# Cross attention of a perceiver block: scores laid out as [key, query] in a ring of seven chunks

## The chip, the cores and the metric

The kernel runs on one core of a Trainium2 chip. The metric is the device time of one launch in microseconds (us). The engines are named as the profile names them: PE (TensorE), DVE (VectorE), ACT (ScalarE), POOL (GpSimd) and SP (the queue that issues the DMAs).

## The reference, cut to what matters

A perceiver block: cross attention of 2 x 128 query tokens over 2 x 2048 context tokens, then self attention, then a feed-forward layer with one of four experts for each token. Everything is float32. The change touches only the first line.

```python
# x: (2, 128, 512)   ctx: (2, 2048, 512)   16 heads of 32
q = split_heads(layernorm(x) @ Wq + bq)
k = split_heads(ctx @ Wk + bk)
v = split_heads(ctx @ Wv + bv)
scores = einsum('bhqd,bhkd->bhqk', q, k) / sqrt(32)
attn = softmax(scores, axis=-1)                  # over 2048 keys
x = x + einsum('bhqk,bhkd->bhqd', attn, v) ... @ Wo + bo
x = x + self_attention(layernorm(x))             # not touched
x = x + ffn(layernorm(x))                        # not touched
```

## The kernel before, in words

Each engine has its own program, written out by hand in one block (`block.tensor`, `block.vector`, `block.scalar`, `block.gpsimd`, `block.sync`); semaphores with constant counts tie them together. An engine works strictly in the order of its program.

The cross attention works in passes `p` = 0 to 7: sample `b = p // 4` and head group `g = p % 4`, four heads to a group. A pass goes over `C` = 4 chunks of 512 keys; chunk number `n = 4p + c` runs from 0 to 31. For a chunk PE does the following:

- `keys` (its products are recorded at L720, in `product`): 12 matmuls of 512 columns make the keys of the four heads from the context, whose float32 values are split in a high and a low part. DVE adds the bias and puts them in `Kr` (L458).
- `scores` (L761): one matmul for each head with the queries stationary. The result is [query, key], 128x512 for a head, in PSUM banks 0 to 3. DVE (`negative_scores`, L478) copies it negated into `Pm` and carries a running minimum of each query, a value of its partition.
- After the four chunks of a pass ACT (`exponentials`, L317) takes the exponent over 2048 keys at once, with the maximum as a bias of the partition, and sums it on the way into `den`.
- `probs_T` (L775): 16 transposes for each chunk turn the probabilities into [key, query]. ACT copies three heads of each chunk into `PT` (L325), DVE the fourth (L487).
- `weighted_values` (L790): 16 matmuls with the values of 32 columns stationary, one column group of PE for each head. `reciprocals_T` (L798), a copy by ACT (L333) and `outputs` (L506, L508) on DVE divide by the sum and write `attnT`.
- `values` (also L720): 48 matmuls for a chunk make the values of all heads. This is done once for a sample: for sample 0 beside pass 0's chunks, for sample 1 in one piece after pass 3 (`if p == G`).

PE interleaves pass `p`'s keys and scores with pass `p - 1`'s transposes and weighted values. POOL splits the context of sample 1 (cast L290, subtraction L292), each chunk as soon as SP has loaded it; SP loads it once PE has used sample 0's chunk for the last time. POOL clears `KM` (L295) after the last weighted values. Then PE multiplies `attnT` by `Wo` (first product from 360.5 us in the profile), and the self attention and the feed-forward layer follow. DVE's step that adds the output's bias row (L567) waits for its row in `rowsA`.

Records: one float32 matmul stands in the trace as two (x2), a transpose and a matmul in the split form as one.

Of the kernel before, what the change touches and what calls it, by code (L numbers as in the profile page):

```python
# [23 lines left out]
def perceiver_block(nc, a, out):  # L24
# [23 lines left out]
    with ExitStack() as ctx:  # L48
# [220 lines left out]
        def _(pool):  # L269
            pool.memset(ident[:], 0.0).then_inc(ident_done, 1)  # L270
            pool.memset(minus_half, -0.5).then_inc(half_done, 1)
# [14 lines left out]
            pool.wait_ge(v_mm, C * JT)  # L286
            for c in range(C):

                pool.wait_ge(raw_in[c], 32)
                pool.tensor_copy(ctxH[c][:], raw[c][:]).then_inc(ctx_hi1, 1)  # L290
                pool.wait_ge(ctx_hi1, c + 1)
                pool.tensor_tensor(ctxL[c][:], raw[c][:], ctxH[c][:].bitcast(F32), ALU.subtract).then_inc(ctx_split1, 1)  # L292

            pool.wait_ge(pv_mm, NP * C)
# [743 lines left out]
```

## Time and profile before

| | |
|---|---|
| runs shown | 608.54, 610.73, 613.24 us; median 610.73 us |
| the profiled execution | 611.93 us, span 610.2 us |
| PE, busy | 540.0 us (88%) |
| DVE, busy | 306.8 us (50%) |
| ACT, busy | 156.8 us (26%) |
| POOL, busy | 35.6 us (6%) |
| mean granted clock of PE | 0.929 of full speed |

The span goes from the first to the last instruction; the run's own time is 1.7 us longer. Busy shares are averages over stages with different limits, so the stage that the change touches, from about 40 to 360 us, has to be read by itself.

### The profile page before, as it was taken

The page shows a single profiled execution, that of the slowest core. Times are in us where ns is not written, and L with a number is a line of the kernel's source. Part 1 is how long each engine was busy: PE and PEld are TensorE (multiplying, and loading weights), DVE is VectorE, ACT ScalarE, POOL GpSimd, SP SyncE. Part 2 cuts the span into 40 slices and gives each one's busy share as a digit, 9 for nine tenths or more (in the row PEclk, how much of TensorE's full clock was granted, in tenths as well). Part 3 has the DMA queues.
Part 4 walks back from the last instruction along what each step waited for, and adds up shares of the span by engine and source line. Part 5 has one row for each costly group of instructions (what it writes and reads, how often), then busy time and mean ns, then how long its engine had stood idle before and what let it go on. Part 6 is the DMA issues. An engine that isn't in the chain of part 4 may idle for free.

```text
span 610.2 us, 8249 instructions
## 1 busy us (share of the span) xinstructions
PE 540.0 (88%) x3378; PEld 389.9 (64%) x3378; DVE 306.8 (50%) x541; ACT 156.8 (26%) x229; POOL 35.6 (6%) x30
## 2 busy tenths in 40 slices
PE   1999999999989899999998778955875999999995
PEld 1777777777767688777775543422735688888642
DVE  6355435556666411175757133184366669766122
ACT  2010034647363431136373610012101100000400
POOL 0000000001950000000000020000000000000000
PEclk9999999999999999999999678975785599999998
DMA  8300000003400000300006240440130475553000
GB/s 355 161 1 0 2 0 2 1 2 118 160 1 3 1 0 1 137 3 2 1 1 275 106 139 1 103 106 0 22 116 0 188 295 165 212 184 129 1 1 33
DMA packets 24620, 46.18 MB, mean 76 GB/s; under 512 B 17540, under 2 KB 17540, under 8 KB 20356
## 3 DMA queue, kind: packets, MB, share of 16 engines
q1 hardware_dynamic: 24584, 45.66, 21.2%
q8 instruction: 27, 0.44, 0.3%
q14 instruction: 9, 0.07, 0.0%
HBM read 43.04 MB, written 2.62 MB: 75 GB/s over the span
## 4 chain that ended last, share of the span: by engine, by line
PE 82%; DVE 9%; DMA 3%; issue 3%; ACT 2%; POOL 0%; POOLq 0%; DVEq 0%; ACTq 0%
PE ps L720 42%; PE ps L775 10%; PE ps L761 6%; PE ps L971 5%; PE ps L790 5%; PE ps L972 5%; PE ps L973 5%; PE ps L906 1%; PE ps L960 1%; DMA qkvp<-qkv_dram 1%; DMA wk_raw<-in_xWk 1%; DVE Pm L478 1%; ACT Pm L317 1%; DVE small L436 1%; PE ps L714 1%
## 5 line engine op out<-in xcount | busy, mean ns | idle before, releaser
L325 ACT COPY PT<-ps 128x512 f32<-128x512 f32 x96 | 53.3, 588 | 99.9 <-PE ps L775 99.9
L775 PE MATMUL ps<-ident,Pm 128*128 128x128 f32 x512 | 72.0, 284 | 3.9 <-ACT PT L325 2.2
L775 PEld LDWEIGHTS ps<-ident,Pm 128*128 128x128 f32 x512 | 58.4, 144 | 24.3 <-issue 16.9
L478 DVE TENSOR_SCALAR_CACHE_REDUCE Pm<-ps,small 128x512 f32<-128x512 f32 x96 | 66.4, 748 | 8.6 <-PE ps L761 8.6
L317 ACT ACTIVATE Pm<-Pm,small 128x2048 f32<-128x2048 f32 x32 | 64.2, 2006 | 14.2 <-DVE Pm L478 14.2
L720 PE MATMUL ps<-ctxH,wkH 128*128 128x512 f32 x128 | 54.0, 422 | 15.3 <-DVE ctxL L450 12.8
L720 PE MATMUL ps<-ctxL,wkH 128*128 128x512 f32 x128 | 51.2, 400 | 0.0
L720 PE MATMUL ps<-ctxH,wkL 128*128 128x512 f32 x128 | 50.9, 398 | 0.0
L971 PE MATMUL ps<-w1H,zH 128*128 128x512 f32 x128 | 50.8, 397 | 0.0
L973 PE MATMUL ps<-w1H,zL 128*128 128x512 f32 x128 | 50.5, 395 | 0.0
L972 PE MATMUL ps<-w1L,zH 128*128 128x512 f32 x128 | 50.5, 395 | 0.0
L720 PE MATMUL ps<-wvH,ctxH 128*128 128x512 f32 x128 | 50.0, 391 | 0.0
L720 PE MATMUL ps<-wvH,ctxL 128*128 128x512 f32 x128 | 49.8, 389 | 0.0
L720 PE MATMUL ps<-wvL,ctxH 128*128 128x512 f32 x128 | 49.8, 389 | 0.0
L458 DVE TENSOR_SCALAR Kr<-ps,small 128x512 f32<-128x512 f32 x32 | 24.0, 750 | 49.2 <-PE ps L720 49.2
L720 PEld LDWEIGHTS ps<-ctxH,wkH 128*128 128x128 f32 x128 | 24.5, 192 | 34.0 <-issue 29.1
L467 DVE COPY V<-ps 128x512 f32<-128x512 f32 x16 | 11.1, 692 | 66.6 <-PE ps L720 66.6
L487 DVE COPY PT<-ps 128x512 f32<-128x512 f32 x32 | 22.1, 692 | 36.7 <-PE ps L775 35.9
L761 PE MATMUL ps<-Kr,qT 32*128 32x512 f32 x256 | 36.5, 640 | 0.6 <-ACT qT L344 0.6
L632 DVE TENSOR_TENSOR w1L<-w1raw,w1H 128x2048 fp32r<-128x2048 f32 x16 | 36.7, 2293 | 0.6
L790 PE MATMUL ps<-PT,V 128*32 128x128 f32 x1024 | 34.9, 277 | 0.9 <-DVE PT L487 0.9
L630 DVE CAST w1H<-w1raw 128x2048 fp32r<-128x2048 f32 x16 | 19.6, 1224 | 24.4 <-PE ps L973 24.4
(138 smaller groups left out, 677.8 us busy)
## 6 DMA issues: line engine op xcount, KB each, us to landing
w1raw<-in_W SPq DMA_DIRECT2D x16, 1024.0 KB, 4.8
raw<-in_ctxT SPq DMA_DIRECT2D x8, 1024.0 KB, 5.8
woF<-in_ffn_Wo SPq DMA_DIRECT2D x1, 4096.0 KB, 14.9
rows<-in_rows SPq DMA_DIRECT2D x8, 256.0 KB, 4.9
qkv_dram<-qkvn SPq DMA_DIRECT2D x2, 768.0 KB, 3.6
qkvp<-qkv_dram SPq DMA_DIRECT2D x2, 768.0 KB, 5.8
wk_raw<-in_xWk SPq DMA_DIRECT2D x1, 1024.0 KB, 4.8
wv_raw<-in_xWv SPq DMA_DIRECT2D x1, 1024.0 KB, 8.5
```

Source lines behind the costliest of these rows:

```text
L317: act.activation(Pm[:, i, :], Pm[:, i, :], ACT.Exp, bias=mx[:, p % 2, i, C - 1:C], scale=-1.0, accum_out=den[:, p, i:i + 1]).then_inc(exp_ ...
L325: act.copy(PT[:, c % 2, i, :, :].rearrange("p k t -> p (k t)"), ps[:, T_BANKS[i % 2], :]).then_inc(pt_act, 1)
L458: dve.tensor_scalar(Kr[:, c, :], ps[:, K_BANK, :], bias3[:, 1, p % G:p % G + 1], None, ALU.add).then_inc(k_done, 1)
L478: dve.tensor_scalar(Pm[:, i, c * CH:(c + 1) * CH], ps[:, i, :], -1.0, mx[:, p % 2, i, c - 1:c] if c else NOT_YET, ALU.mult, ALU.min, accum ...
L632: dve.tensor_tensor(w1L[n % 2][:], w1raw[n % 2][:], w1H[n % 2][:].bitcast(F32), ALU.subtract).then_inc(w1_split, 1)
L720: mm = pe.matmul(dst, l, r, start=(n == 0), stop=(n == len(pairs) - 1))
L761: pe.matmul(ps[:, i, :], qT[q, g, b * T:(b + 1) * T], Kr[q, c, :], start=True, stop=True)\
L775: last = pe.transpose(ps[:, T_BANKS[i % 2], j * P:(j + 1) * P], Pm[:, i, c * CH + j * P:c * CH + (j + 1) * P], ident[:])
L790: last = pe.matmul(ps[q, PV_BANK, 0:T], V[:, c * JT + j, (HPG * g + i) * DH:(HPG * g + i + 1) * DH], PT[:, c % 2, i, j, :], start=(c == 0 ...
L971: pe.matmul(dst, zH[:, n, t], wH[:, cc], start=False, stop=False)
L972: pe.matmul(dst, zH[:, n, t], wL[:, cc], start=False, stop=False)
L973: last = pe.matmul(dst, zL[:, n, t], wH[:, cc], start=False, stop=(n == NW1 - 1))
```

## The change

The work of a chunk is laid out as [key, query], so that the probabilities need no transposes.

- PE `scores`: the keys are stationary, 128 of them at a time, and the 128 queries of a head move: 16 matmuls of 128 columns for a chunk in place of 4 of 512. ACT, not DVE, copies the result into one of seven buffers `Sm` (8 KB each per partition), and ACT, not DVE, adds the bias to the keys; `Kr` has two buffers.
- The maximum of a query now lies over partitions. DVE `running_max` reduces a chunk's four blocks of 128 keys by a strided view into [128 keys, head, query] and takes the maximum with the chunks before. At the end of a pass PE transposes it (`maxima_T`), DVE reduces it to one value a query and head (`maxima`), PE spreads it over all partitions (`maxima_rows`, four matmuls with a broadcast column as weights), and ACT copies it to `mb`.
- DVE `subtract` takes `mb` from a whole chunk (128x2048), ACT takes the exponent of the chunk in place, PE multiplies it with the values.
- The sums of the probabilities: in the passes of `POOLED` POOL adds a chunk's four blocks into `acc` (three adds for chunk 0 of a pass, four for chunks 1 and 2), and PE adds chunk 3 and `acc` over the partitions with `ones` as weights (20 matmuls). In passes 2 and 7 PE does it all with `ones` (16 matmuls more a chunk). DVE takes the reciprocal of 128 columns.
- All engines now go through slots `n` = 0 to 37. In slot `n` PE makes scores `n`, keys `n + 1` and weighted values `n - 6`; ACT takes the exponent of `n - 6` and copies scores `n`; DVE takes the maximum of `n - 1` and subtracts for `n - 5`. The values of sample 1 are made in slots 19 to 22, one chunk in each.
- `acc` and `tmp` lie where `x` lay, so SP loads `x` again near the end of the stage.

The core of the diff:

```diff
-PT = at("PT", [P, 2, HPG, JT, T], F32, 160)
-Kr = at("Kr", [P, C, CH], F32, 176)
+NS = 7
+Sm = [at(f"Sm{n}", [P, HPG, JT, T], F32, 128 + 8 * n) for n in range(NS)]
+Kr = at("Kr", [P, 2, CH], F32, 184)
+run = at("run", [P, HPG, T], F32, 188)
+mb = at("mb", [P, HPG, T], F32, 190)
+acc = at("acc", [P, HPG, T], F32, 192)
+tmp = at("tmp", [P, HPG, T], F32, 194)
 x = at("x_sb", [P, B, D], F32, 192)
 qT = at("qT", [P, G, TOK], F32, 196)
 attnT = at("attnT", [P, G, TOK], F32, 200)
 ident = at("ident", [P, P], F32, 204)
 RT = at("RT", [P, T], F32, 204.5)
...
 NP = B * G
-NOT_YET = 3.0e38
+NCH = NP * C
+LAG = 6
+M_BANK, DEN_BANK = T_BANKS
+V1_SLOT = (G - 1) * C + LAG + 1
+POOLED = (0, 1, 3, 4, 5, 6)
...
+def pooled(n):
+    return n // C in POOLED and n % C < C - 1
+def denominator(p):
+    return ps[:, PV_BANK, P:2 * P] if p in POOLED else ps[:, DEN_BANK, 0:T]
+def sums_through(n):
+    return sum(pooled(k) for k in range(n + 1))
+def sums_before(p):
+    return sum(q < p for q in POOLED)
...
         sp.dma_start(w1raw[n][:], w1_v[n]).then_inc(w1_in[n], 16)
-    sp.wait_ge(s_mm, NP * C * HPG)
+    sp.wait_ge(s_mm, NCH * HPG)
     for n in range(2):
         sp.dma_start(rowsA[:, n, :], a["rows"][n:n + 1, :].to_broadcast([P, D])).then_inc(rowsA_in, 16)
+    sp.wait_ge(mT_mm, NP)
+    sp.wait_ge(den_mm, len(POOLED))
+    sp.dma_start(x[:], a["x"].rearrange("b t d -> t b d")).then_inc(x_in, 16)
+    sp.wait_ge(pv_mm, NCH)
     sp.dma_start(wr[:], a["W_router"]).then_inc(wr_in, 16)
-    sp.wait_ge(pv_mm, NP * C)
     for n in range(8):
         sp.dma_start(rows[:, n, :], a["rows"][2 + n:3 + n, :].to_broadcast([P, D])).then_inc(rows_in, 16)
...
+    steps = [0]
+    def denominators(n):
+        t = Sm[n % NS]
+        before = sums_through(n) - 1
+        pool.wait_ge(exp_done, n + 1)
+        if before:
+            pool.wait_ge(summed, before)
+        if n % C == 0:
+            if sums_before(n // C):
+                pool.wait_ge(den_mm, sums_before(n // C))
+            pool.tensor_tensor(acc[:], t[:, :, 0, :], t[:, :, 1, :], ALU.add).then_inc(add_step, 1)
+            steps[0] += 1
+        else:
+            for j in range(2):
+                pool.tensor_tensor(acc[:], acc[:], t[:, :, j, :], ALU.add).then_inc(add_step, 1)
+                steps[0] += 1
+                if j == 0:
+                    pool.wait_ge(add_step, steps[0])
+        pool.wait_ge(add_step, steps[0])
+        pool.tensor_tensor(acc[:], acc[:], t[:, :, 2, :], ALU.add).then_inc(add_step, 1)
+        steps[0] += 1
+        pool.wait_ge(add_step, steps[0])
+        pool.tensor_tensor(acc[:], acc[:], t[:, :, 3, :], ALU.add).then_inc(summed, 1)
+    for n in range(NCH):
+        if n == 2 * C:
+            pool.wait_ge(v_mm, C * JT)
+            for c in range(C):
+                pool.wait_ge(raw_in[c], 32)
+                pool.tensor_copy(ctxH[c][:], raw[c][:]).then_inc(ctx_hi1, 1)
+                pool.wait_ge(ctx_hi1, c + 1)
+                pool.tensor_tensor(ctxL[c][:], raw[c][:], ctxH[c][:].bitcast(F32),
+                                   ALU.subtract).then_inc(ctx_split1, 1)
+        if pooled(n):
+            denominators(n)
...
+    def keys(n):
+        g = n // C % G
+        act.wait_ge(k_mm, n + 1)
+        if n >= 2:
+            act.wait_ge(s_mm, (n - 1) * HPG)
+        act.activation(Kr[:, n % 2, :], ps[:, K_BANK, :], ACT.Identity, bias=bias3[:, 1, g:g + 1],
+                       scale=1.0).then_inc(k_done, 1)
...
+    def scores(n):
+        if n >= NS:
+            act.wait_ge(pv_mm, n - NS + 1)
+            if pooled(n - NS):
+                act.wait_ge(summed, sums_through(n - NS))
+            if (n - NS) % C == C - 1 and (n - NS) // C in POOLED:
+                act.wait_ge(den_mm, sums_before((n - NS) // C) + 1)
+        for i in range(HPG):
+            act.wait_ge(s_mm, n * HPG + i + 1)
+            act.copy(Sm[n % NS][:, i, :, :].rearrange("p j t -> p (j t)"), ps[:, i, :]).then_inc(s_done, 1)
+    def maxima(p):
+        act.wait_ge(mB_mm, p + 1)
         if p:
...
+            act.wait_ge(sub_done, C * p)
+        act.copy(mb[:].rearrange("p h t -> p (h t)"), ps[:, M_BANK, :]).then_inc(mb_done, 1)
+    def exponentials(n):
+        act.wait_ge(sub_done, n + 1)
+        t = Sm[n % NS][:].rearrange("p h j t -> p (h j t)")
+        act.activation(t, t, ACT.Exp).then_inc(exp_done, 1)
+    act.wait_ge(bias_in, 16)
...
+    for n in range(NCH + LAG):
+        if n >= LAG:
+            exponentials(n - LAG)
+        if n < NCH:
+            scores(n)
+        if C < n <= NCH + 1 and n % C == 1:
+            maxima(n // C - 1)
+        if n + 1 < NCH:
+            keys(n + 1)
+        if n + 1 < C:
+            for j in (0, 2):
+                values(0, n + 1, j)
...
+    def running_max(n):
+        t = Sm[n % NS]
+        dve.wait_ge(s_done, HPG * (n + 1))
+        dst = tmp if n % C else run
+        if n:
+            dve.wait_ge(run_ready, n)
+        red = dve.tensor_reduce(dst[:], t[:].rearrange("p h j t -> p h t j"), AX.X, ALU.max)
+        if n % C == 0:
+            red.then_inc(run_ready, 1)
+            return
+        run_steps[0] += 1
+        red.then_inc(run_step, 1)
+        dve.wait_ge(run_step, run_steps[0])
+        dve.tensor_tensor(run[:], run[:], tmp[:], ALU.max).then_inc(run_ready, 1)
+    def maxima(p):
+        dve.wait_ge(mT_mm, p + 1)
+        dve.tensor_reduce(mq, ps[:, M_BANK, :].rearrange("p (h t) -> p h t", h=HPG), AX.X, ALU.max)\
+           .then_inc(m_ready, 1)
+    def subtract(n):
+        t = Sm[n % NS]
+        dve.wait_ge(mb_done, n // C + 1)
+        dve.tensor_tensor(t[:], t[:], mb[:].rearrange("p h (o t) -> p h o t", o=1).to_broadcast([P, HPG, JT, T]),
+                          ALU.subtract).then_inc(sub_done, 1)
     def outputs(p):
         b, g = divmod(p, G)
         dst = attnT[:, g, b * T:(b + 1) * T]
...
         dve.wait_ge(pv_mm, C * (p + 1))
...
+        if p in POOLED:
+            dve.wait_ge(den_mm, sums_before(p) + 1)
+        dve.reciprocal(RT[:], denominator(p)).then_inc(o_step, 1)
+        dve.wait_ge(o_step, 2 * p + 1)
+        dve.tensor_tensor(dst, ps[:, PV_BANK, 0:T], RT[:], ALU.mult).then_inc(o_step, 1)
+        dve.wait_ge(o_step, 2 * p + 2)
         dve.tensor_scalar(dst, dst, bias3[:, 2, g:g + 1], None, ALU.add).then_inc(o_done, 1)
...
+    for n in range(NCH + LAG):
+        if n + 1 < C:
+            if n + 2 < C:
+                split(n + 2)
+            for j in (1, 3):
+                values(0, n + 1, j)
+        if 0 <= n - 1 < NCH:
+            running_max(n - 1)
+        if n >= C and n % C == 0 and n <= NCH:
+            maxima(n // C - 1)
+        if n - LAG >= C and (n - LAG) % C == 0:
+            outputs((n - LAG) // C - 1)
+        if 0 <= n - (LAG - 1) < NCH:
+            subtract(n - (LAG - 1))
+        if 0 <= n - V1_SLOT < C:
+            for j in (1, 3):
+                values(1, n - V1_SLOT, j)
     outputs(NP - 1)
...
         t = slice(j * P, (j + 1) * P)
         product(ps[:, T_BANKS[j % 2], :], [(l[:, k, t], w[:, k, :]) for k in range(KT)
                                            for l, w in ((ctxH[c], wvH), (ctxH[c], wvL), (ctxL[c], wvH))])\
...
+    def scores(n):
+        b, g = divmod(n // C, G)
         pe.wait_ge(k_done, n + 1)
+        for j in range(JT):
+            for i in range(HPG):
+                q = slice(DH * i, DH * (i + 1))
+                if n and j == 0:
+                    pe.wait_ge(s_done, (n - 1) * HPG + i + 1)
+                mm = pe.matmul(ps[:, i, j * P:(j + 1) * P], Kr[q, n % 2, j * P:(j + 1) * P],
+                               qT[q, g, b * T:(b + 1) * T], start=True, stop=True)
+                if j == JT - 1:
+                    mm.then_inc(s_mm, 1)
...
+    def values_made(slot):
+        return 2 * C + 2 * max(0, min(C, slot - V1_SLOT))
+    def maxima_T(p, slot):
+        pe.wait_ge(run_ready, C * (p + 1))
+        pe.wait_ge(v_act, values_made(slot))
+        if p:
+            pe.wait_ge(mb_done, p)
         for i in range(HPG):
...
+    def maxima_rows(p, slot):
+        pe.wait_ge(m_ready, p + 1)
+        pe.wait_ge(v_act, values_made(slot))
+        for i in range(HPG):
+            last = pe.matmul(ps[:, M_BANK, i * P:(i + 1) * P], mq[:, i:i + 1].to_broadcast([P, P]), ident[:],
+                             start=True, stop=True)
+        last.then_inc(mB_mm, 1)
+    def weighted_values(n):
+        p, c = divmod(n, C)
+        pe.wait_ge(exp_done, n + 1)
+        if p % G == 0:
+            pe.wait_ge(v_act, 2 * (C * (p // G) + c + 1))
+            pe.wait_ge(v_dve, 2 * (C * (p // G) + c + 1))
         if c == 0 and p:
...
+            pe.wait_ge(o_done, p)
         g = p % G
+        t = Sm[n % NS]
         for j in range(JT):
             for i in range(HPG):
                 q = slice(DH * i, DH * (i + 1))
                 last = pe.matmul(ps[q, PV_BANK, 0:T], V[:, c * JT + j, (HPG * g + i) * DH:(HPG * g + i + 1) * DH],
...
+                                 t[:, i, j, :], start=(c == 0 and j == 0), stop=(c == C - 1 and j == JT - 1))
+        if p not in POOLED:
+            for j in range(JT):
+                for i in range(HPG):
+                    last = pe.matmul(denominator(p)[DH * i:DH * (i + 1)], ones[:], t[:, i, j, :],
+                                     start=(c == 0 and j == 0), stop=(c == C - 1 and j == JT - 1))
         last.then_inc(pv_mm, 1)
...
+        if c == C - 1 and p in POOLED:
+            pe.wait_ge(summed, sums_through(n))
+            for i in range(HPG):
+                den = denominator(p)[DH * i:DH * (i + 1)]
+                for j in range(JT):
+                    pe.matmul(den, ones[:], t[:, i, j, :], start=(j == 0), stop=False)
...
     pe.wait_ge(wk_split, 1)
...
+    keys(0)
     pe.wait_ge(wv_split, 1)
...
+    pe.wait_ge(ones_set, 1)
+    for n in range(NCH + LAG):
+        if n < NCH:
+            scores(n)
+        if C < n <= NCH + 1 and n % C == 1:
+            maxima_rows(n // C - 1, n)
+        if n + 1 < NCH:
+            keys(n + 1)
+        if n >= C and n % C == 0 and n <= NCH:
+            maxima_T(n // C - 1, n)
+        if n + 1 < C:
+            for j in range(JT):
+                values(0, n + 1, j)
+        if 0 <= n - V1_SLOT < C:
+            for j in range(JT):
+                values(1, n - V1_SLOT, j)
+        if n >= LAG:
+            weighted_values(n - LAG)
     pe.wait_ge(wo_in, 16)
...
+    pe.wait_ge(o_done, NP)
+    pe.wait_ge(s_done, NCH * HPG)
     for b in range(B):
         product(ps[:, b, :], [(attnT[:, k, b * T:(b + 1) * T], wo[:, k, :]) for k in range(KT)])\
             .then_inc(wo_mm, 1)
...
```

## Rows read from the trace of the kernel before

**Rows 1.** The page: the chain that ended last, by engine.
```profile
PE 82%; DVE 9%; DMA 3%; issue 3%; ACT 2%; POOL 0%; POOLq 0%; DVEq 0%; ACTq 0%
```

**Rows 2.** Busy time by stretch: window, its us, each engine's busy time, granted clock, DMA.
```profile
118.00:146.00 28.00, 27.94 (x275) 20.32 (x274) 17.34 (x44) 14.68 (x22) 0.00 (x0) 1.00 0.01 2
204.00:251.00 47.00, 46.75 (x206) 38.43 (x206) 6.26 (x12) 12.95 (x17) 0.00 (x0) 1.00 0.04 12
333.00:360.00 27.00, 17.17 (x208) 12.80 (x196) 8.49 (x21) 15.12 (x22) 3.19 (x1) 0.80 0.33 125
```

**Rows 3.** The chain in order of time: start us, length us, what.
```profile
84.84 1.07 PE ps L761 x8
...
118.22 2.77 PE ps L720 x12
...
125.77 1.07 PE ps L761 x8
...
127.86 1.01 PE ps L790 x32
128.88 1.02 PE ps L775 x8
...
146.41 2.77 PE ps L720 x12
...
204.59 46.28 PE ps L720 x204
...
360.50 10.07 PE ps L720 x16
```

**Rows 4.** Groups of instructions, each shape apart: busy us, mean ns, idle before.
```profile
L317 ACT ACTIVATE Pm<-Pm,small 128x2048 f32<-128x2048 f32 x32 | 64.2, 2006 | 14.2 <-DVE Pm L478 14.2
...
L325 ACT COPY PT<-ps 128x512 f32<-128x512 f32 x96 | 53.3, 588 | 99.9 <-PE ps L775 99.9
...
L632 DVE TENSOR_TENSOR w1L<-w1raw,w1H 128x2048 fp32r<-128x2048 f32 x16 | 36.7, 2293 | 0.6
...
L292 POOL TENSOR_TENSOR ctxL<-raw,ctxH 128x2048 fp32r<-128x2048 f32 x4 | 18.3, 4573 | 0.3
...
L607 DVE TENSOR_REDUCE small<-ps 128x4 f32<-128x512 f32 x8 | 5.5, 692 | 12.1 <-PE ps L906 12.1
...
L281 POOL TENSOR_TENSOR small<-small 128x1 f32<-128x1 f32 x10 | 5.5, 549 | 260.3 <-DVE small L438 260.3
...
L344 ACT ACTIVATE qT<-ps,small 128x256 f32<-128x256 f32 x4 | 1.9, 474 | 5.8 <-PE ps L720 5.8
...
L644 DVE TENSOR_TENSOR u<-u,rows 128x512 f32<-128x512 f32 x2 | 1.4, 693 | 0.1
...
L621 DVE RECIPROCAL small<-ps 128x16 f32<-128x16 f32 x2 | 0.5, 254 | 6.3 <-PE ps L890 6.3
```

**Rows 5.** Timeline of ACT: start us, us, engine line op [idle before].
```profile
121.47 1.07 ACT L325 COPY PT<-ps 128x512 f32<-128x512 f32 x2 [0.58 <-PE ps L775]
```

**Rows 6.** Timeline of the weight loads.
```profile
430.60 3.65 PEld L890 LDWEIGHTS ps<-V,PT 128*128 128x128 f32 x32
```

**Rows 7.** Timeline of DVE beside POOL.
```profile
149.92 1.90 POOL L290 CAST ctxH<-raw 128x2048 fp32r<-128x2048 f32 x1 [128.04 <-DMA raw<-in_ctxT]
...
150.21 1.69 DVE L508 TENSOR_SCALAR attnT<-attnT,small 128x128 f32<-128x128 f32 x1
...
171.36 4.58 POOL L292 TENSOR_TENSOR ctxL<-raw,ctxH 128x2048 fp32r<-128x2048 f32 x1
...
172.27 0.75 DVE L478 TENSOR_SCALAR_CACHE_REDUCE Pm<-ps,small 128x512 f32<-128x512 f32 x1
...
172.94 0.18 DVE L493 RECIPROCAL small<-small 128x4 f32<-128x4 f32 x1
...
173.15 2.87 DVE L497 COPY rexp<-small 128x128 f32<-128x128 f32 x1
...
357.81 2.59 DVE L508 TENSOR_SCALAR attnT<-attnT,small 128x128 f32<-128x128 f32 x1
```

More of the change, by code:

```diff
@@ L284, in _ @@
                 rsqrt(b)
[L286 to L294, printed above, removed]
+            steps = [0]
[32 more added lines that the diff above has]
+                    denominators(n)
+            pool.wait_ge(pv_mm, NCH)
             pool.memset(KM[:], 0.0).then_inc(km_zero, 1)
@@ L482, in probs_T @@
[L482 to L498 removed]
+            run_steps = [0]
@@ L721, in product, with keys @@
                 return mm
-            def keys(p, c):
+            def keys(n):
+                p, c = divmod(n, C)
                 b, g = divmod(p, G)
@@ L764, in probs_T @@
-            def probs_T(p, c, i):
-                pe.wait_ge(exp_done, HPG * p + i + 1)
-                n = p * C + c
-                if i == 0 and n:
-                    pe.wait_ge(pt_act, 3 * n)
-                if i == 1 and n:
-                    pe.wait_ge(pt_dve, n)
-                if i >= 2:
-                    pe.wait_ge(pt_act, 3 * n + i - 1)
-                for j in range(JT):
-                    last = pe.transpose(ps[:, T_BANKS[i % 2], j * P:(j + 1) * P],
-                                        Pm[:, i, c * CH + j * P:c * CH + (j + 1) * P], ident[:])
-                last.then_inc(t_mm, 1)
@@ L815, in _ @@
             pe.wait_ge(q_done, G)
-            scores(0, 0)
-            for c in range(1, C):
-                keys(0, c)
-                for j in range(JT):
-                    values(0, c, j)
-                scores(0, c)
-            for p in range(1, NP + 1):
-                more = p < NP
-                late = p >= 2 and p != G + 1
-                if more:
-                    keys(p, 0)
-                if late:
-                    weighted_values(p - 2, C - 1)
-                    reciprocals_T(p - 2)
-                if more:
-                    keys(p, 1)
-                if p == 1 or p == G + 1:
-                    pe.wait_ge(v_act, p // G * 2 * C + 2 * C)
-                    pe.wait_ge(v_dve, p // G * 2 * C + 2 * C)
-                for c in range(C):
-                    probs_T(p - 1, c, 0)
-                    probs_T(p - 1, c, 1)
-                    if c == 0 and more:
-                        keys(p, 2)
-                    if c:
-                        weighted_values(p - 1, c - 1)
-                    probs_T(p - 1, c, 2)
-                    probs_T(p - 1, c, 3)
-                    if more:
-                        scores(p, c)
-                        if c == 1:
-                            keys(p, 3)
-                if p == G:
-                    weighted_values(p - 1, C - 1)
-                    reciprocals_T(p - 1)
-                    for c in range(C):
-                        for j in range(JT):
-                            values(1, c, j)
```

177 lines of the change are left out of this document (25 added, 152 removed).

## The prediction

> **What bounds the kernel now.** First the chain by engine: PE holds 82% of it [rows 1]. Averages over the span say little for a change to one stage, so next the busy times by stretch [rows 2]. From 118 to 146 us, one pass, PE is busy for 27.94 of 28 us and DVE for 17.34 of them, ACT for 14.68, POOL for nothing; the same holds while sample 1's values are made (204 to 251). Only at the stage's end (333 to 360) does PE fall to 17.2 of 27 us and its clock to 0.80. So until 333 us the stage is PE's own work. The chain in order of time [rows 3] gives its terms: the pass that begins at 118.22 is followed by the next at 146.41, a period of 28.2 us. In it: keys 4 x 2.8 to 3.0, scores 4 x 1.07, weighted values 4 x 1.01, transposes 8 x 1.02. The 8.2 us of transposes are what the change takes out. The last scores of pass 0 start at 84.84 and the product with Wo starts at 360.50: 275.7 us that the sum below replaces. What lies before and behind stays.
>
> **PE after the change.** Gone: transposes, 8.2 us a pass. Added in a pass: the maximum's transposes (4, about 0.5) and its spreading (8 records of 128 columns, 0.9), the sums (40 records for a pooled pass, 1.3; 4.0 in passes 2 and 7, at 1.01 for 16 matmuls [rows 3]). Scores: the columns that move are as many (16 x 128), so 1.07 a chunk is the low end; weight loads are four times as many. A load of 128 columns costs 3.65/32 = 0.11 us [rows 6]; eight rounds of four head groups at 0.11 behind eight rounds of 0.107 are 1.7, the high end. I take 1.2, near the low end, because loads overlap matmuls in every row of rows 3 (keys, 12 in 2.8 us). PE then has 4 x (1.2 + 2.8 + 1.0) + 2.7 = 22.7 us a pass. Were PE still the bound, a pass would gain 5.5 us.
>
> **DVE after the change.** Gone: 16 L478, 4 L458, 4 L487. Added: a reduction and a subtraction over 2048 columns for each chunk. A reduction of 512 takes 0.69 like a tensor_tensor of 512, and a tensor_tensor of 2048 takes 2.29 [rows 4]; I take 2.3 for both. The trace has no reduction whose inner step is 128 elements; low end 2.3, high end twice that (see the rivals). Then three maxima of 0.7 (L644's shape), one reduction of 0.7, and outputs: a reciprocal of 128 columns, (254 - 175)/12 = 6.6 ns a column between 16 columns [rows 4] and 4 columns [rows 7], so 1.0, and two operations of 128 columns, 0.3 each when not held. Sum: 9.2 + 9.2 + 2.1 + 0.7 + 1.6 = 22.8 us a pass. It is as long as PE's.
>
> **ACT.** Four score copies a chunk (588 ns each alone, two in 1.07 [rows 4, 5], so four in 2.1), the exponent 1.9 (2006 ns with its sum), the keys with bias 0.7 (474 ns for 256 columns): 4.7 a chunk, and 0.6 a pass for `mb`: 19.4 us.
>
> **POOL.** 11 adds of 512 columns for a pooled pass. Ends: 4573/4 = 1.14 us, and a line through 549 ns for one column and 4573 for 2048, 1.55 [rows 4]. The 549 is a power, dearer than an add, so I take 1.25, and 0.08 between two: 5.3 us for four adds, 14.6 a pass.
>
> **No engine is full, but they wait for each other.** I follow DVE through the four slots of a pass, from the end of its slot `n % 4 == 1`:
> - slot 2: running maximum 3.0, outputs 1.6, subtraction 2.3: 6.9;
> - slot 3: 3.0 + 2.3: 12.2;
> - slot 0: running maximum to 15.2; `maxima_T` stands in PE's queue behind scores and keys and gives its result at about 16.4; reduction 0.7, subtraction: 19.4. In DVE's queue the subtraction is stuck behind this wait, 1.2 us;
> - slot 1: the subtraction needs `mb`. ACT copies `mb` only after the exponent of the chunk just subtracted (1.9) and four score copies (2.1): 24.0. Subtraction: 26.3.
>
> So 26.3 us a pass if nothing else comes in, 1.9 less than 28.2.
>
> **DVE and POOL beside each other** [rows 7]. A DVE operation from SBUF to SBUF that began while POOL worked ended only with POOL: 1.69 and 2.59 us for 128 columns at L508, 2.87 at L497, about 0.3 otherwise, and each ended within 0.1 us of POOL's. One that reads PSUM (L478, 0.75) and a reciprocal of 4 columns (0.18) were not held. The subtractions and running maxima read two tiles in SBUF. The trace has none of these beside POOL, so the ends are 0 and a whole add each. Of the large SBUF to SBUF operations that it shows beside POOL all were held; I take it that these are too. POOL's adds (14.6 us) and DVE's subtractions and maxima (11.3) then need 25.9 us one after the other, and that only if neither ever comes at a bad time. The walk again, with the adds of chunk `c` starting when its exponent ends:
> - slot 2: the add of chunk 0 holds the maximum by 0.7, another holds the last step of outputs by 1.0: 8.6;
> - slot 3: the maximum held by 0.7: 14.6; POOL has two of chunk 1's four adds left;
> - slot 0: the sum of chunk 1 is done at 18.9, the reduction of the maximum too; the subtraction and the first add of chunk 2 contend: 21.2 to 22.3;
> - slot 1: `scores` on ACT may write only in a buffer whose sum is done. POOL ends chunk 2 at 26.4, where the exponent had ended at 23.5. Copies 28.5, `mb` 29.1, subtraction 31.3.
>
> 31.3 us a pass, 3.1 more than now. In pass 2 POOL makes no sums but splits the context (4 x (1.9 + 4.6) us). Each subtraction or maximum may now meet 4.6 us: by the same walk 38 us.
>
> The Trainium skill (SBUF — State Buffer, Who interferes with whom) says that a DVE instruction with two SBUF inputs and a POOL instruction that reads SBUF exclude each other for a whole instruction, and that a tensor_reduce on trn2 never does. The trace agrees for one-input operations (2.87 us); it has no two-input one beside POOL. By the rule the second walk stands; without it the first.
>
> **The sum.** From 84.8: slots 3 to 5 have no exponents, and a slot is scores and keys, 4.2, and a key copy that nothing hides, 0.9: they start at 84.8, 89.9 and 95.0. In slot 5 scores end at 96.3, the copies at 98.5, `mb` at 99.1, the subtraction at 101.4. Passes to 132.7 and 164.0, pass 2 to 202. Slots 19 to 22 start at 209.5, and there PE is the bound: 46.28 us for 204 matmuls is 0.227 each, 48 of them are 10.9, plus 1.2 + 2.7 + 1.0 = 15.8 each, to 272.7. Slots 23 to 31 at the pace above end at 341.0. The tail: maxima and first subtraction 348.1; exponent, `mb`, subtraction 352.9; outputs and three subtractions 361.4; exponent 1.9; weighted values with `ones` 2.2: 365.5; reciprocal and product 366.8; the last addition is held by POOL's clearing of KM as it is now (2.59 [rows 7]): 369.3. Wo starts at 369.8, 9.3 later than now. 611.9 + 9.3 = 621.2 on the profiled execution's own time; it lies 1.2 over the median, so 620.0 as a median. The reload of x (512 KB) starts some 20 us before it is needed, the start with keys on ACT has PE as its bound for pass 0's values: 0 each, and some 5 us if x came late.
>
> **Rivals.**
> 1. *The two-input operations are not held.* Passes of 26.3: marks at 101.4, 154.0, 180.3 (the splits keep ahead of the keys), 185.5 to 248.7 with the values, 306.3 for slot 31, Wo at 335.2. 25.3 us less than now: 585.4 as a median. For: POOL has 12 us free a pass; the small reciprocal was not held. Against: L508, L497.
> 2. *Held, but it costs half*, because waiting adds fill gaps that DVE has anyway (3.5 us a pass in the first walk): some 29.5 a pass, 33 in pass 2, so 4.5 x 1.8 + 5 = 13 us less than the sum, 607: no change.
> 3. *The strided reduction runs slower*: at half rate 2.3 us more a chunk on DVE, the longest queue; about 7 of the 9.2 us a pass come through, in four and a half passes beside the one walk or the other: 651, or 617 with nothing held. The Trainium skill (Advanced Engine Details and Errata, Memory Cachelines) says that an access that crosses to a new 16-byte line each time pays a penalty; here every read does, at a step of 512 bytes. No row here shows one.
> 4. *The clock.* In the second walk PE ends its keys in slot 2 at 2.7 and waits until 6.4 for `outputs`. Between 333 and 360, with PE busy for 17 of 27 us, the clock went below full [rows 2]. Keys and scores of one slot at 1.2 in place of 2.4 GHz (4.0 us more, of which some 3.3 reach DVE's next wait), five times: 637. With adds of 1.55 us it is about the same, 636.
>
> **How the numbers follow.** The forecast (held, 608 to 637) 0.42; rival 1, 0.28; rival 2, 0.16; rivals 3 and 4, 0.14. A measurement of this kernel tells about 1% from no change. The forecast's lower edge and rival 2 give same 0.17; rival 1 and a little of rival 2 give faster 0.31; the rest, 0.52, is slower. The likeliest case alone has 608 to 640. The range must take in most of rival 1 and the clock: 583 to 643.
>
> **What would show it.** Subtractions on DVE with a mean above 2.6 us and running maxima above 0.9 (held) or at 2.29 and 0.69 (rival 1); reductions of 2048 at 2.3 or 4.5 (rival 3); a period of 31, 29 or 26 us between first weighted values of passes 4 to 6; PE below 80% busy in them; ACT's first score copy in slot 1 waiting for POOL; PE's clock in a pass (rival 4). The forecast is wrong if PE is still over 95% busy in a pass.

## The result: 649.0 us, 6% slower

The changed kernel takes 649.0 us (median of 4 runs, 648.70 to 649.82) against 610.96 (608.54 to 613.24): the recorded ratio is 1.0605, 95% interval 1.0554 to 1.0656 (the two medians alone give 1.062). Of the runs used below one is left out: the sixth of e11 took 642.98 us at a granted clock of 0.808, where its others had 0.933 to 0.947. The forecast was 620.0 with a range to 643. The direction was right, the size was outside the range. The profiled execution took 649.82, its span is 648.0; before they were 611.93 and 610.2.

The page of after, busy time in 40 slices of 16.2 us, and the granted clock:
```profile
PE   2899978696868899998869267875796699999995
...
DVE  6233379999899954459999973336436758776322
...
PEclk9999998889788899999989787997558689999999
```
DVE is busy for 80% or more of slices 7 to 14 and 19 to 23; PE in most of them is not. The chain that ended last, by engine, answers to [rows 1]:
```profile
PE 53%; DVE 30%; issue 10%; ACT 4%; DMA 2%; POOL 0%; POOLq 0%; ACTq 0%; DVEq 0%
```
DVE has 30% where it had 9%. Busy times of one pass of about 34 us (window, its us, PE, weight loads, DVE, ACT, POOL, granted clock, DMA, GB/s), which answer to [rows 2]:
```profile
310.00:344.00 34.00, 26.69 (x355) 21.58 (x354) 32.00 (x16) 18.48 (x26) 16.98 (x11) 0.90 0.01 1
```
DVE works for 32.0 of 34 us. PE's share fell from all of the pass to 78%, as the forecast had it. The chain in order of time (start, length, what), which answers to [rows 3]:
```profile
255.90 1.10 PE ps L797 x32
...
315.21 3.87 DVE tmp L527
...
321.96 2.29 DVE Sm L546
324.25 3.86 DVE tmp L527
328.13 1.35 DVE run L534
...
332.69 3.73 DVE tmp L527
...
336.44 1.52 DVE run L534
...
338.01 1.13 PE ps L813 x4
...
398.75 9.75 PE ps L756 x16
```
Wo's product starts at 398.75; it started at 360.50. These 38.2 us are the whole difference of the spans (37.8). The chain runs through the running maximum (L527 and L534) and the subtraction (L546), chunk after chunk. Scores take 1.10 us. The reduction that `maxima` makes once a pass (L539) is used below as the mark of a pass: the marks of passes 1 and 2 lie 34.4 us apart. The groups, each shape apart (busy us, mean ns, idle before and its releaser), which answer to [rows 4]:
```profile
L527 DVE TENSOR_REDUCE tmp<-Sm 128x512 f32<-128x2048 f32 x24 | 91.7, 3823 | 0.2
...
L546 DVE TENSOR_TENSOR Sm<-Sm,mb 128x2048 f32<-128x2048 f32 x32 | 86.5, 2710 | 6.2 <-ACT mb L397 6.2
...
L403 ACT ACTIVATE Sm<-Sm 128x2048 f32<-128x2048 f32 x32 | 61.3, 1914 | 93.2 <-DVE Sm L546 93.2
...
L534 DVE TENSOR_TENSOR run<-run,tmp 128x512 f32<-128x512 f32 x24 | 33.3, 1387 | 0.8
...
L328 POOL TENSOR_TENSOR acc<-acc,Sm 128x512 f32<-128x512 f32 x24 | 30.6, 1275 | 47.7 <-ACT Sm L403 46.8
```
The reduction takes 3.82 us, not 2.3. The subtraction (2.71) and the maximum (1.39) lie above the 2.29 and 0.69 of such shapes alone, so they are held. DVE's pass by these rows: 4 x 3.82 + 4 x 2.71 + 3 x 1.39 + 0.7 + 1.6 = 32.6 us, against 32.0 in the window. How the holding looks in the timeline of DVE beside POOL (start, length, engine, line):
```profile
144.34 1.30 POOL L333 TENSOR_TENSOR acc<-acc,Sm 128x512 f32<-128x512 f32 x1
...
144.75 1.44 DVE L534 TENSOR_TENSOR run<-run,tmp 128x512 f32<-128x512 f32 x1
...
154.66 1.61 POOL L333 TENSOR_TENSOR acc<-acc,Sm 128x512 f32<-128x512 f32 x1
...
155.06 3.37 DVE L546 TENSOR_TENSOR Sm<-Sm,mb 128x2048 f32<-128x2048 f32 x1
...
156.35 3.21 POOL L336 TENSOR_TENSOR acc<-acc,Sm 128x512 f32<-128x512 f32 x1
```
The maximum that comes at 144.75 ends at 146.19, 0.55 us behind POOL's end at 145.64, as if nearly all of its 0.69 us lay behind it. The subtraction that comes at 155.06 ends at 158.43, 2.16 us behind POOL's end at 156.27, and POOL's next add ends 1.13 us behind the subtraction: it takes 3.21 us in place of 1.27. Each engine stops the other.

### The profile page after: what moved, and what is told of

Its sections match the earlier page's. It is cut to its first block, busy times and chain, and to the rows that moved or that the text cites. A ratio compares the mean times of both kernels' runs of the same rounds, so it can differ in the third digit from the quotient of the medians.

```text
span 648.0 us, 9478 instructions
## 1 busy us (share of the span) xinstructions
PE 529.4 (82%) x4210; PEld 401.6 (62%) x4210; DVE 420.0 (65%) x309; ACT 186.8 (29%) x261; POOL 144.1 (22%) x97
## 4 chain that ended last, share of the span: by engine, by line
PE 53%; DVE 30%; issue 10%; ACT 4%; DMA 2%; POOL 0%; POOLq 0%; ACTq 0%; DVEq 0%
PE ps L756 28%; DVE tmp L527 13%; DVE Sm L546 5%; PE ps L1002 5%; PE ps L1003 5%; PE ps L1004 5%; DVE run L534 4%; ACT Sm L390 2%; PE ps L921 2%; PE ps L797 1%; PE ps L937 1%; PE ps L813 1%; ACT Sm L403 1%; DMA qkvp<-qkv_dram 1%; DVE RT L556 1%
## 5 line engine op out<-in xcount | busy, mean ns | idle before, releaser
L527 DVE TENSOR_REDUCE tmp<-Sm 128x512 f32<-128x2048 f32 x24 | 91.7, 3823 | 0.2
L546 DVE TENSOR_TENSOR Sm<-Sm,mb 128x2048 f32<-128x2048 f32 x32 | 86.5, 2710 | 6.2 <-ACT mb L397 6.2
L403 ACT ACTIVATE Sm<-Sm 128x2048 f32<-128x2048 f32 x32 | 61.3, 1914 | 93.2 <-DVE Sm L546 93.2
L390 ACT COPY Sm<-ps 128x512 f32<-128x512 f32 x128 | 65.4, 597 | 35.1 <-PE ps L797 35.1
L839 PE MATMUL ps<-Sm,V 128*32 128x128 f32 x1024 | 39.5, 301 | 20.9 <-DVE attnT L560 13.8
L839 PEld LDWEIGHTS ps<-Sm,V 128*32 128x32 f32 x1024 | 29.3, 119 | 31.6 <-issue 21.0
L797 PE MATMUL ps<-qT,Kr 32*128 32x128 f32 x1024 | 43.8, 315 | 4.5 <-ACT Kr L369 3.9
L324 POOL TENSOR_TENSOR acc<-Sm 128x512 f32<-128x512 f32 x6 | 7.7, 1291 | 171.7 <-ACT Sm L403 137.3
L797 PEld LDWEIGHTS ps<-qT,Kr 32*128 32x128 f32 x1024 | 37.1, 215 | 13.4 <-issue 6.5
L328 POOL TENSOR_TENSOR acc<-acc,Sm 128x512 f32<-128x512 f32 x24 | 30.6, 1275 | 47.7 <-ACT Sm L403 46.8
```

The source lines that it names most:

```text
L328: pool.tensor_tensor(acc[:], acc[:], t[:, :, j, :], ALU.add).then_inc(add_step, 1)
L390: act.copy(Sm[n % NS][:, i, :, :].rearrange("p j t -> p (j t)"), ps[:, i, :]).then_inc(s_done, 1)
L403: act.activation(t, t, ACT.Exp).then_inc(exp_done, 1)
L527: red = dve.tensor_reduce(dst[:], t[:].rearrange("p h j t -> p h t j"), AX.X, ALU.max)
L546: dve.tensor_tensor(t[:], t[:], mb[:].rearrange("p h (o t) -> p h o t", o=1).to_broadcast([P, HPG, JT, T]), ALU.subtract).then_inc(sub_don ...
L797: mm = pe.matmul(ps[:, i, j * P:(j + 1) * P], Kr[q, n % 2, j * P:(j + 1) * P], qT[q, g, b * T:(b + 1) * T], start=True, stop=True)
```

## Experiments: the two costs apart

The theory was: 3.82 is the price of the 512-byte step, and it and the holding by POOL together make the loss. The rivals: only one of the two matters; or what is gained on DVE comes back as another wait (`mb` behind ACT's copies, PE, the clock). The first four are single runs and share a single run of before (613.22).

**e1_contig.** The reduction reads runs of four neighbours. It has as many elements in and out, but the maxima are those of other elements, so this is an experiment and not a version to use:
```
-dve.tensor_reduce(dst[:], t[:].rearrange("p h j t -> p h t j"), AX.X, ALU.max)
+dve.tensor_reduce(dst[:].rearrange("p h t -> p (h t)"),
+    t[:].rearrange("p h j (x y) -> p (h j x) y", y=JT), AX.X, ALU.max)
```


> The running maximum is reduced over four neighbouring queries instead of the four key blocks: the same 2048 columns in and 512 out, but every read is next to the last one (the maxima are those of other elements; only the view differs). Theory stride (the step of 512 bytes makes the reduction slow): the reduction falls from 3.82 to about 2.3 us, the pass period from 34 to about 31 us, the whole to 625 to 632 us. Theory count (a reduction with four elements to an output costs 3.8 us however it reads): it stays at 3.82 and the time at 649 us.

Measured: 626.1 us, 22.9 less than after. Its groups and its chain in order of time (two reciprocals, one pass apart):
```profile
L527 DVE TENSOR_REDUCE tmp<-Sm 128x512 f32<-128x2048 f32 x24 | 54.6, 2276 | 0.2
...
L535 DVE TENSOR_TENSOR run<-run,tmp 128x512 f32<-128x512 f32 x24 | 37.0, 1541 | 0.8
```
```profile
302.48 0.96 DVE RT L557
...
320.09 3.24 POOL acc L333
323.40 1.31 POOL acc L336
...
325.26 1.57 ACT Sm L390 x3
...
333.44 0.95 DVE RT L557
```
With 2.28 us in place of 3.82 the pass takes 31.0 us. The forecast's second walk, made with 2.3 and with holding, said 31.3, and the path is the one that it walked: POOL's last adds of chunk 2, then ACT's score copies, then `mb` and the subtraction. Since the number of elements is unchanged, 1.5 us of the reduction are the price of the step.

**e2_pesums.** POOL adds only in the two passes whose sums can't lie on PE for want of a bank; PE does the others:
```
-POOLED = (0, 1, 3, 4, 5, 6)
+POOLED = (3, 4)
```


> Passes 0, 1, 5 and 6 get their sums on PE with ones, as 2 and 7 do; POOL adds only in passes 3 and 4. Theory hold (adds on POOL and two-input operations on DVE exclude each other): subtractions beside no POOL work go to 2.29 us and maxima to 0.69, in these passes the period falls from 34 to about 31 us, the whole to 635 to 640 us. Theory stride alone: DVE's 29 us a pass of its own work stay the bound, the mean durations fall but the whole stays within 5 us of 649, or rises, because PE gets 2.7 us more a pass.

Measured: 630.71 us, 18.3 less than after. Its groups:
```profile
L527 DVE TENSOR_REDUCE tmp<-Sm 128x512 f32<-128x2048 f32 x24 | 91.7, 3823 | 0.2
...
L534 DVE TENSOR_TENSOR run<-run,tmp 128x512 f32<-128x512 f32 x24 | 23.8, 992 | 0.8
```
The maximum falls from 1.39 to 0.99 us: in passes 0, 1, 5 and 6 nearly all take 0.69, and the longer ones (up to 3.14) stand beside the split of the context and in passes 3 and 4. The time lies 4 us under the range expected. The reduction stays at 3.82 with POOL and without: this operation with one input is not held, although a copy (L497) and the addition of a bias (L508) were in the kernel before [rows 7].

**e4_contig_pesums.** Both edits.

> Both first edits: contiguous reduction (maxima of other elements) and sums on PE in passes 0, 1, 5, 6. This is the first walk of the prediction, nothing held and reductions of 2.3 us: 26.3 us a pass in passes 1, 5 and 6, the whole about 600 to 606 us. If stride and hold do not add (each hides the other), the period stays near 29 to 30 us and the whole at 620 to 628 us.

Measured: 612.96 us, 36.0 less than after, 5.2 short of the two parts' sum (41.2), and 7 over the 606 that was expected at most. Part of what DVE saves comes back as its wait for `mb`: 6.2 us in all in after, 6.1 in e2, 18.5 in e1 and 16.1 here. The split still costs: the marks of passes 2 and 3 lie 39.5 us apart. Its chain in order of time, and its windows:
```profile
293.04 2.29 DVE tmp L527
...
297.71 1.08 PE ps L840 x32
...
319.71 2.29 DVE tmp L527
```
```profile
293.00:320.00 27.00, 26.02 (x473) 21.44 (x465) 22.23 (x17) 18.70 (x26) 0.00 (x0) 1.00 0.01 2
```
A pass of 26.7 us; the forecast's first walk, with nothing held, said 26.3. PE is back at 26.0 of 27 us and at full clock, and the chain runs through it for some 12 us from 297.71 on. With all sums on PE its own work is about as long as the walk of DVE, so this run does not test the 26.3 by itself. The two edits take back 36 of the 38 us, though e2's part gives PE the sums of four more passes.

**e3_pair.** No reduction over a chunk: the running maximum as a chain of two-input maxima of 512 columns, each waiting for the one before:
```
-red = dve.tensor_reduce(dst[:], t[:].rearrange("p h j t -> p h t j"), AX.X, ALU.max)
+for j in range(1 if n % C == 0 else 0, JT):
+    mx = dve.tensor_tensor(run[:], first, t[:, :, j, :], ALU.max)
+    first = run[:]
+    ...
+        dve.wait_ge(run_step, run_steps[0])
```


> The reduction over the four key blocks and the maximum with the chunks before become four (three in chunk 0) two-input maxima of 512 columns with contiguous reads, same result. Alone: 15 x 0.69 = 10.4 us a pass in place of 17.4. If holding by POOL's adds is small, the period falls by about 6 us (34 to 28), the whole to about 605 us. If each of the 15 now waits for half an add (0.6), 9 us come back: the period stays at 33 to 35 and the whole at 640 to 655 us.

Measured: 657.23 us, 8 more than after. Its group:
```profile
L528 DVE TENSOR_TENSOR run<-run,Sm 128x512 f32<-128x512 f32 x112 | 129.6, 1157 | 3.3
```
Alone such a maximum takes 0.7, four 2.9, less than 3.82; here the mean is 1.16, so four take 4.6 where the reduction and the maximum that they replace took 5.2. What is left of the gain comes back as DVE's wait for `mb` (13.7 us in all, 6.2 in after). The 8 us that are lost on top lie in one place, beside the split: the marks of passes 2 and 3 are 50.0 us apart, where after has 37.6, while the marks of passes 1 and 2 (33.8), 5 and 6 (34.3) lie as in after (34.4 both).

## Experiments: a version that gives the right maximum without either cost

The runs of before for these have a median of 610.44 (e5, e6, e8, e9), and 609.94 (e7, e10, e11, e12). e5, e7, e9 and e12 are single runs.

**e5_pair_pesums.** e3 with e2's edit.

> Contiguous two-input maxima in place of the strided reduction, result unchanged, and sums on PE in passes 0, 1, 5, 6. Theory hold: with no adds beside them the maxima go to 0.69 us, 10.4 us a pass, less than the 11.3 of the kernel with contiguous reductions and sums on PE (612.96 us), so the whole is 608 to 616 us. If two-input operations cost more than 0.69 for a reason other than POOL, the mean stays near 1.16 us and the whole above 635 us.

Measured: 624.29 us, a miss by 8: with POOL's sums gone, the split of sample 1's context still stood on POOL in pass 2 (47.7 us between the marks of passes 2 and 3). **e6_pair_pesums_mb** moves `mb` ahead of the exponent and the score copies in ACT's queue as well:
```
+if C < n <= NCH + 1 and n % C == 1:
+    maxima(n // C - 1)
 exponentials(n - LAG)
 scores(n)
-if C < n <= NCH + 1 and n % C == 1:
-    maxima(n // C - 1)
```


> The same with one more edit: ACT copies mb before the exponent and the four score copies of its slot, not after. Theory wait chain (the subtraction of the next pass waits for that copy): the 2.4 us of DVE idle before it go, in 5 or 6 of the 8 passes and once at the end, so 10 to 16 us less than the run without it, 596 to 604 us. If PE (25 us of work a pass and keys behind ACT's key copy) is late next, only 3 to 6 us less.

Measured: 618.54 us, ratio 1.0128 (1.0111 to 1.0144): 5.7 less than e5, and again too slow by 14. DVE's wait for `mb` fell by more, from 14.0 to 3.4 us; where POOL does nothing the chain runs through PE (25.6 us between the marks of passes 1 and 2). Where the rest is lost, the timeline of e6 shows (POOL, then DVE in the same stretch and DVE later):
```profile
159.12 6.43 POOL L346 TENSOR_TENSOR ctxL<-raw,ctxH 128x2048 fp32r<-128x2048 f32 x1
...
161.11 12.92 DVE L528 TENSOR_TENSOR run<-run,Sm 128x512 f32<-128x512 f32 x4
...
177.66 2.86 DVE L528 TENSOR_TENSOR run<-run,Sm 128x512 f32<-128x512 f32 x4
```
Beside the split four maxima take 12.9 us; without, 2.86. The marks of passes 2 and 3 lie 48.2 us apart.

**e7_mb** is after with this move alone.

> The changed kernel with one edit: ACT copies mb ahead of the exponent and the score copies. In the changed kernel DVE stands still before that subtraction for 6.2 us in all, since its strided reduction of 3.8 us fills the wait. Theory DVE full: 2 to 6 us less than 649. Theory wait chain (the copy order sets the pass even here): 12 us less or more.

Measured: 646.1 us, 2.9 less. DVE's wait for `mb` fell from 6.2 us to 1.1:
```profile
L546 DVE TENSOR_TENSOR Sm<-Sm,mb 128x2048 f32<-128x2048 f32 x32 | 86.7, 2714 | 1.1 <-ACT mb L397 1.1
```
That the order in ACT's queue makes the loss would have given 12 us or more, so this rival falls; 2.9 us from a single run is itself less than before's runs differ (4.7). The order comes to matter once the reduction is short (18.5 us of waits in e1).

**e8_tj_act** and **e9_tj_pe** keep the right reduction and let it read neighbours, by storing the scores query by query with the four key tiles inside (both with e2's and e6's edits). In e8 ACT's copy writes with a step of 16 bytes, in e9 PE does when it writes the scores; in both PE reads the probabilities with a step of 16 bytes:
```
-Sm = [at(f"Sm{n}", [P, HPG, JT, T], F32, 128 + 8 * n) for n in range(NS)]
+Sm = [at(f"Sm{n}", [P, HPG, T, JT], F32, 128 + 8 * n) for n in range(NS)]
-dve.tensor_reduce(dst[:], t[:].rearrange("p h j t -> p h t j"), AX.X, ALU.max)
+dve.tensor_reduce(dst[:], t[:], AX.X, ALU.max)
# e9 only
-mm = pe.matmul(ps[:, i, j * P:(j + 1) * P], ...
+mm = pe.matmul(ps[:, i, :].rearrange("p (t j) -> p t j", j=JT)[:, :, j], ...
```


> A chunk is kept as [key, head, query, block], so that the reduction reads its four elements side by side, with the same result; ACT's score copies write with a step of 16 bytes and PE reads the probabilities with that step. Sums on PE in passes 0, 1, 5, 6 and mb copied early, as in the run before. Theory DVE only (the step costs only DVE's reads in the reduction): reductions 2.28 us, copies 0.6, weighted values 1.0, the whole 596 to 606 us. If ACT's writes or PE's reads pay too, weighted values go from 1.0 towards 2 us and the whole to 620 us or more.

> The same layout, but PE writes the scores with a step of 16 bytes into PSUM and ACT copies contiguously. If only DVE's reductions mind a step: as the run before, 596 to 606 us. If PE's writes into PSUM pay, scores take 2 us or more a chunk in place of 1.10.

Measured: 649.2 us (ratio 1.0629, 1.0597 to 1.0661) and 641.81, both missed by some 40. The groups of e8:
```profile
L390 ACT COPY Sm<-ps 128x512 f32<-128x512 f32 x128 | 122.8, 1123 | 45.2 <-PE ps L797 45.2
...
L839 PE MATMUL ps<-Sm,V 128*32 128x128 f32 x1024 | 64.8, 407 | 12.6 <-DVE attnT L560 9.8 <-ACT Sm L403 2.7
...
L527 DVE TENSOR_REDUCE tmp<-Sm 128x512 f32<-128x2048 f32 x24 | 54.8, 2282 | 23.4 <-ACT Sm L390 23.2
```
and the chain of e9 in order of time:
```profile
333.66 1.95 PE ps L839 x32
335.61 1.84 PE ps L844 x32
337.45 1.10 PE ps L797 x32
```
and a window of e9:
```profile
290.00:330.00 40.00, 40.00 (x491) 27.62 (x492) 30.53 (x18) 22.40 (x30) 13.10 (x6) 1.00 0.07 28
```
The reduction is at 2.28, as wanted. But ACT's copy of 512 columns went from 0.60 to 1.12 us, and PE's reading with a step from 1.01 [rows 3] to 1.95 us a chunk (L839, at full clock both times), and the sums from 0.87 to 1.84 (L844). PE is busy all of the 40 us: it is the bound, and four times 1.9 us more a pass is what the marks of passes 1 and 2 show (32.8 us, where e6 has 25.6). Only PE's writing with a step cost nothing: scores stay at 1.10. The layout moves the stride's price from DVE to engines that pay more for it.

**e10_split** is e6 with the split of sample 1's context taken from POOL: ACT makes `ctxH` in slots 13 to 16, DVE `ctxL` one slot later.
```
+if 0 <= n - (LAG + 7) < C:
+    act.copy(ctxH[c][:], raw[c][:]).then_inc(ctx_hi1, 1)
 ...
+if 0 <= n - (LAG + 8) < C:
+    dve.tensor_tensor(ctxL[c][:], raw[c][:], ctxH[c][:].bitcast(F32), ALU.subtract)...
```


> Pairwise maxima, sums on PE in passes 0, 1, 2, 5, 6, 7, mb copied early (618.5 us with these three), and the split of sample 1's context moved from POOL to ACT and DVE. There each maximum beside POOL's split took 4.9 us in place of 0.7 and pass 2 some 38 us. Theory hold: pass 2 becomes DVE's 22 us and 9.2, about 31 us; less 1 or 2 us of waits: 608 to 613 us. If the two new steps come late for PE's keys, 615 to 620 us.

Measured: 600.85 us (597.79 to 604.09), ratio 0.9834 (0.9794 to 0.9873): 17.7 less than e6 and 7 under the range expected. The expectation took pass 2 of e6 as 38 us; between the marks of passes 2 and 3 it is 48.2, and 28.0 in e10. 7.2 us of that gain come back between the next two marks. **e11_only3** leaves POOL the sums of pass 3 alone, PE takes pass 4's too, waiting for the values' bank.
```
-POOLED = (3, 4)
+POOLED = (3,)
+if p == G and c == 0:
+    pe.wait_ge(v_dve, 4 * C)
```


> As the run before, and pass 4's sums on PE too (with a wait until its bank is free of values), so that POOL adds only in pass 3, where PE's values set the pace. Theory hold: the maxima of 1.7 us and the subtractions of over 3 us in slots 23 to 25 go back to 0.7 and 2.3, 5 to 7 us less than the run before: 602 to 607 us, faster than the kernel before. If that stretch is PE's own by then (24.5 us a pass), 1 to 3 us less.

Measured: 597.6 us (median of five, 595.86 to 602.16), ratio 0.9807 (0.9776 to 0.9837): faster than both kernels, by 1.9% against before, and the interval leaves open whether it is 2%. That is 3 us less than e10, as the second alternative had it and not the 5 to 7 of the first; the runs of e10 and e11 overlap, so even this gain is not shown. Its windows and groups:
```profile
105.00:130.00 25.00, 24.64 (x443) 20.49 (x432) 18.86 (x24) 18.29 (x25) 0.00 (x0) 1.00 0.01 3
...
281.00:305.00 24.00, 23.62 (x395) 19.32 (x395) 19.41 (x23) 18.46 (x25) 0.00 (x0) 1.00 0.01 3
```
```profile
L523 DVE TENSOR_TENSOR run<-run,Sm 128x512 f32<-128x512 f32 x112 | 84.7, 756 | 8.4 <-ACT Sm L381 5.2
L542 DVE TENSOR_TENSOR Sm<-Sm,mb 128x2048 f32<-128x2048 f32 x32 | 74.0, 2319 | 3.5 <-ACT mb L388 3.4
```
PE is the bound again (24.64 of 25 us, 23.62 of 24), at full clock, and hardly anything is held any more (0.76 and 2.32 us). The chain in order of time, score copies one pass apart:
```profile
123.70 1.94 ACT Sm L381 x4
...
149.32 1.94 ACT Sm L381 x4
```
The pass takes 25.6 us. The forecast's PE work for a pass, 22.7 with pooled sums and 2.7 more with all sums on PE, is 25.4.

**e12_after_split** is after with e10's edit alone.

> The changed kernel with one edit: POOL no longer splits the context of sample 1; ACT casts it (2 us a chunk, in slots 13 to 16) and DVE subtracts (2.3 us a chunk, in slots 14 to 17). Theory hold: the split blocks DVE's two-input operations for 4.6 us at a time, and pass 2 takes 38 us where the others take 34; without it pass 2 is DVE's own work, 29 us and 9.2 more, with no holds: 38 again, so the whole stays within 3 us of 649. If POOL's split cost nothing, DVE's 9.2 us more would show: 656 us or more.

Measured: 646.7 us, 2.3 less, from a single run. While POOL's adds and the slow reduction stay, moving the split is worth almost nothing: the marks of passes 2 and 3 lie 34.6 us apart in place of 37.6, and the next two 43.5 in place of 40.5. Between e6 and e10 it is worth 17.7. But that is not one cost coming out from behind two others: the pairwise maxima made the split dearer. Time between marks, us:

| marks of passes | after | e1 | e2 | e3 | e4 | e6 | e10 | e11 | e12 |
|---|---|---|---|---|---|---|---|---|---|
| 1 and 2 | 34.4 | 31.3 | 29.9 | 33.8 | 26.6 | 25.6 | 25.6 | 25.6 | 33.9 |
| 2 and 3 (split) | 37.6 | 40.2 | 38.3 | 50.0 | 39.5 | 48.2 | 28.0 | 28.0 | 34.6 |
| 3 and 4 | 40.5 | 37.8 | 40.5 | 41.1 | 39.3 | 37.5 | 44.7 | 45.0 | 43.5 |
| 5 and 6 | 34.4 | 30.2 | 30.8 | 34.3 | 27.6 | 28.1 | 28.0 | 25.6 | 34.1 |

With the reduction and the split on POOL (after, e1, e2, e4) the second row is 38 to 40 us; with pairwise maxima (e3, e6) it is 48 to 50. The split moved beside e4's edits was not run.

## Why the prediction was wrong in size and right in direction

**The step that failed** is the DVE term "a tensor_tensor of 2048 takes 2.29; I take 2.3 for both", for subtraction and reduction. The reduction with an inner step of 128 elements takes 3.82 us, 1.5 more a chunk. The bounds, 2.3 and twice that, held it; the value was taken at the low end, by the nearest row, though no row had that step. Undone alone (e1) it gives back 22.9 us, to 626.1: that is inside the range and 6 over the forecast, and still 2% over the run of before beside it (613.22), so the direction does not hang on the missed term.

**What is left of the miss** has its largest part in a term for PE. In e1 the product with `Wo` starts at 378.06, 8.3 us behind the 369.8 of the sum. Slots 19 to 22, put at 4 x 15.8 = 63.2 us, last from 207.43 to 275.88, 68.5 us:
```profile
207.43 1.10 PE ps L798 x32
...
257.77 0.88 PE ps L853 x10
...
260.90 1.10 PE ps L798 x32
...
262.00 13.88 PE ps L757 x60
```
The sum had nothing there for what PE does once a pass: transposes 0.7, spreading 1.1, and the sums of a pooled pass, which take 3.1 us (257.77 to 260.90) where the working had 1.3.

**Rival 3** had the mechanism and the total (651), but it took the reduction at half rate, 2.3 us more a chunk, and 1.5 was measured. With 1.5 its own working gives some 21 us more than 620, 641; that it lies 2 us from 649.0 is in part luck. It let 7 of 9.2 us through; what came through depended on what else a pass waits for. The once-a-pass reduction (L539 of after, its counterpart in e1) starts at 100.37 and 94.59 in pass 0, at 130.37 and 118.62 in pass 1: 5.8 and 6.0 us more, nearly the whole 6.2 (4 x 1.55) each time, since DVE alone sets these. In the next four passes only 3.1, -2.6, 2.7 and 1.6 us come through, and 4.3 and 2.6 in the last two. The Trainium skill (Advanced Engine Details and Errata, Memory Cachelines) says that reads which go to a different 16-byte line of SBUF each time pay a penalty. The traces agree for this reduction: 3.82 us at a step of 512 bytes (after) against 2.28 with neighbours (e1).

**Held by POOL** (rivals 1 and 2 against the forecast): right. The forecast took it from one-input operations [rows 7] and gave the second walk 31.3 us a pass; with the reduction at 2.3 it is 31.0 (e1). The first walk's 26.3 stands beside 26.7 in e4, but there PE sets as much of the pass as DVE does. The prediction says that the trace had no two-input operation beside POOL; it had one, L567, which began at 358.01 and took 2.39 us where 0.69 is usual. It stood behind the held L508 and ended with it, so it shows no holding of its own. Rival 2, half a cost, falls. Subtraction above 2.6 (2.71) and maximum above 0.9 (1.39) are as listed. Rival 1's 585 for the whole was not reached by e4 (613.0), where POOL still splits the context and adds in passes 3 and 4: its marks (L540) lie 39.5 and 39.3 us apart there, and 26.6, 27.6 and 25.5 in the passes without. The listed wait of ACT's first score copy for POOL is not in after (0 in all passes); in e1, with the shorter reduction, it is there, about 0.65 us in each of six places.

**PE**: scores 1.10 (1.2 taken, ends 1.07 and 1.7), maximum's transposes 0.67 (0.5), spreading 1.09 (0.9): right; sums of a pooled pass 3.1 (1.3): too low. PE is below 80% busy, as listed.

**ACT and POOL**: four copies 2.03 (2.1), exponent 1.91 (1.9), keys 0.70 (0.7), add 1.27 (1.25): right.

**The clock** (rival 4) went to 0.90 in the pass, and back to 1.00 where PE was full (e4, e11). In after it cost little, since DVE worked for 32 of the 34 us: on the chain that ended last, pieces at a granted clock of 0.50 (1.2 GHz) are the maximum's transposes in four passes (1.12 or 1.13 us in place of 0.67) and scores in two slots (2.06 and 2.02 in place of 1.10), 3.7 us together, where the rival had 17. No run separates it.

**Pass 2**, put at 38 us against 31.3 for others: 37.6 between the marks of passes 2 and 3 in after, 40.2 in e1. The reload of x is not on the chain.

## What to carry to other kernels

When a change moves work to an engine that until then had slack, time the new operation in its own access pattern before anything else: a row of equal size with neighbouring elements was 1.5 us short of 3.8, on the engine that became the bound. Count SBUF to SBUF operations with two inputs on DVE and POOL as one queue, and move POOL's share away before tuning either. Ask of a repair what it makes dearer: four short maxima in place of one long reduction were cheaper alone and raised the price of the split, from 38 to 40 us between two marks to 48 to 50, until the split was moved too.

## What the hardware showed that was not expected

- A step inside an SBUF access has a price of its own on each of three engines: DVE's reduction at 512 bytes 3.82 against 2.28 us, ACT's write at 16 bytes 1.12 against 0.60, PE's reading of the moving operand at 16 bytes 1.95 against 1.01 for 16 matmuls. PE's write to PSUM at 16 bytes had none (1.10 both).
- A chain of short two-input operations on DVE, each waiting for the one before, fares worse beside POOL than one long operation: four maxima that take 2.86 us alone took 12.92 beside POOL's casts and subtractions of 2048 columns, one of which took 6.43 in turn where it takes 4.57 alone (e6).
- The two engines hold each other in both directions (POOL's add 3.21 in place of 1.27 us).
